# Graph passes: six of the 416 gathered tiles go through the SyncE queue, row by row

## The chip, the cores and the metric

One NeuronCore of a Trainium2 chip runs the whole program in one launch. The metric is the time of one execution on the device, in microseconds (us), as the median of several runs. PE is TensorE, DVE is VectorE, ACT is ScalarE, POOL is GpSimd, SP is SyncE. SP does no arithmetic here: it issues transfers and waits for semaphores.

## The reference

The model is a chain of four residual blocks over 3125 nodes of 256 features and 53,125 edges. The change is in the third block, a graph network of five layers:

```python
for l in range(L):                      # L = 5
    xl = h @ W[l] + b[l]
    ee = edge_attr @ We[l] + be[l]
    msg = norm * jax.nn.relu(xl[row] + ee)
    agg = jnp.zeros_like(xl).at[col].add(msg)
    conv = agg + jax.nn.relu(xl + root[l]) / deg[:, None]
    ...                                 # batch norm over the nodes, relu, residual
```

Each layer therefore gathers one row of `xl` for each edge (`xl[row]`), adds the edge's own product, and adds the result up by target node.

## The kernel before

The edges are sorted by target and padded to 416 tiles (`ET`) of 128 edges. A layer is one graph pass, `graph_layer_edges`. It has 26 iterations (`ITERS`) of 16 tiles (`BODY`), and the tiles are worked two at a time: pair `u` of an iteration is tiles `2u` and `2u+1`. The first pass ("opening") reads a table of 258 columns (`xl_table`, `XROW`), whose last two columns are weights of the node; the other four read `xl_rows` with 256 columns, and run inside a loop over the layers.

The engines work side by side in one block and are ordered by semaphores that count tiles or pairs:

- POOL, `gather(n)`: for each of the two tiles of pair `n` one indirect transfer fetches 128 rows into buffer `g.g[:, j]`, where `j` is the tile's place in its iteration. There are 16 buffers. From the ninth pair on it first waits until the pair that last used the buffers has been summed (`g.summed`). Its loop is written out in full (208 pairs).
- SP: `load_features` brings the edge features of half an iteration (8 tiles, 512 KB) into `g.ea[:, q]`. The load for half `q` of the next iteration waits until PE has made the products of half `q` of this one (`g.product`), so each load is asked for about half an iteration ahead of its use. The first two loads are made before the pass.
- PE: `products` multiplies the features of a pair with `We` into PSUM, two pairs ahead; `sums` multiplies messages with a one-hot matrix (the sum by target).
- DVE: `add_pair` (L2523) adds gathered rows and product; `add_sums` (L2544) adds the sums to `agg`; once an iteration it loads 16 register values with `lagging_bases` (L154).
- ACT: the relu of the messages and half of the one-hot matrices. In the first pass DVE also copies weights out of the gathered tiles for each half (`keep_half`, `g.kept`), and POOL waits for that copy before it reuses the buffers.

SP's part of the pass is these lines:

```python
with sp.Fori(0, ITERS - 1) as it:
    at = [places(q, it + 1) for q in range(2)]
    used = [sp.snap(it * (BODY // 2) + HALF // 2 * (q + 1)) for q in range(2)]
    for q in range(2):
        sp.wait_ge(g.product, used[q])
        load_features(q, at[q])
```

Of the kernel before, what the change touches and what calls it, by code (L numbers as in the profile page):

```python
# [42 lines left out]
SCORE_WINDOW = 2  # L43
LAYERS = 5
XROW = D + 2
PARTS = 3
EA = PARTS * PARTS * 4
ED = 128
# [1943 lines left out]
def graph_first_inputs(k):  # L1992
# [7 lines left out]
    with ExitStack() as c:  # L2000
# [11 lines left out]
        @block.sync  # L2012
        def _(sp):
            def load_x(i):
                sp.dma_start(k.x[:, i * STEP:(i + 1) * STEP, :], tile_rows(k.sum_d, i * STEP, STEP)).then_inc(x_in[i], 16)

            load_x(0)
            sp.dma_start(w[:], a["g1_w"][0:P, :].rearrange("p (b d) -> p b d", b=K)).then_inc(g.weights, 16)
            sp.dma_start(g.bias[:], a["g1_bias"][0:1, :].broadcast_to([P, 2 * D])).then_inc(g.weights, 16)
            sp.dma_start(g.cols[:], a["g1_cols"][0:P, :]).then_inc(g.weights, 16)  # L2020
            sp.dma_start(g.we[:], a["g1_we"][0:P, :]).then_inc(g.weights, 16)
            for i in range(1, NSTEP):
                load_x(i)
            sp.wait_ge(done, 1)
            sp.dma_start(k.deg_d, k.deg[:]).then_inc(stored, 16)
            load_first_half_tiles(k, sp)
            sp.wait_ge(stored, 16)
            sp.dma_start(k.dinv_row[:, 0:NP], k.deg_d.rearrange("t p -> (t p)").unsqueeze(0).broadcast_to([P, NP])
                         ).then_inc(stored, 16)
            sp.wait_ge(ready, 2)  # L2030
            with nc.allow_non_contiguous_dma(reason="two numbers for each row of the table"):
                sp.dma_start(k.xl_table[:, D:XROW].rearrange("(t p) c -> p t c", p=P), cols[:]
                             ).then_inc(stored, 16)
            for s in range(NSTEP):
                sp.wait_ge(g.biased, STEP * (s + 1))
                sp.dma_start(tile_rows(k.xl_table, s * STEP, STEP, 0, D), row[:, s % 2, :, :]).then_inc(g.stored[s % 2], 16)
            sp.wait_ge(stored, 48)
            for s in range(2):
                sp.wait_ge(g.stored[s], 16 * ((NSTEP + 1 - s) // 2))

# [317 lines left out]
def graph_layer_edges(k, l, nodes=None):  # L2358
# [13 lines left out]
    @block.sync  # L2372
    def _(sp):
        if nodes:
            nodes.sync(sp)

        def places(q, it):
            return a["ea128"][:, bass.ds(it * (BODY * P) + q * HALF * P, HALF * P)]

        def load_features(q, of_ea):  # L2380
            sp.dma_start(g.ea[:, q, :], of_ea).then_inc(g.ea_in[q], 16)

        with sp.Fori(0, ITERS - 1) as it:
            at = [places(q, it + 1) for q in range(2)]
            used = [sp.snap(it * (BODY // 2) + HALF // 2 * (q + 1)) for q in range(2)]
            for q in range(2):
                sp.wait_ge(g.product, used[q])
                load_features(q, at[q])

        for s in g.of_nodes:  # L2390
            sp.sem_clear(s)
        sp.wait_ge(g.added, ET + SB)

    @block.gpsimd
    def _(pool):
        if nodes:
            nodes.gpsimd(pool)

        def gather(n):

            for t in (2 * n, 2 * n + 1):
                j = t % BODY
                nc.gpsimd.indirect_dma_start(  # L2403
                    out=g.g[:, j, 0:width], out_offset=None, in_=table[:, :],
                    in_offset=bass.IndirectOffsetOnAxis(ap=k.src_all[:, t:t + 1], axis=0)
                ).then_inc(g.src_in[j], 16)

        for n in range(ET // 2):
            if n >= BODY // 2:
                pool.wait_ge(g.summed, 2 * (n - BODY // 2 + 1) + BODY)  # L2410
            if opening and n >= BODY // 2 and n % (HALF // 2) == 0:
                pool.wait_ge(g.kept, (n - BODY // 2) // (HALF // 2) + 1)
            pool.sem_inc(g.begun, 1)
            gather(n)
# [93 lines left out]
    def _(dve):  # L2508
# [5 lines left out]
        dve.sem_inc(g.added, SB)  # L2514
        dve.sem_inc(g.started, 2)

        def add_pair(it, u, seen):
            dve.wait_ge(g.product, it * (BODY // 2) + u + 1)
            dve.wait_ge(g.src_in[2 * u], seen)
            dve.wait_ge(g.src_in[2 * u + 1], seen)  # L2520

            dve.wait_ge(g.summed, it * BODY + 2 * u + 2)
            nc.vector.tensor_tensor(g.msg[:, 2 * u:2 * u + 2, :], g.g[:, 2 * u:2 * u + 2, 0:D],  # L2523
                                    ep[u % EB][:, 0:2 * D].rearrange("p (a d) -> p a d", a=2), ALU.add
                                    ).then_inc(g.raw, 1)
# [32 lines left out]
                                        ).then_inc(g.started, 1)  # L2558
                dve.wait_ge(g.started, it * 2 + 4)

        def body(it, first):
            seen = it * 16 + l * (16 * ITERS) + 16
            for u in range(BODY // 2):
                if not opening:
                    dve.wait_ge(g.summed, it * BODY + 2 * u + 2)
                    hot_tile(it, 2 * u)
                add_pair(it, u, seen)
                if opening and u % (HALF // 2) == HALF // 2 - 1:
                    keep_half(it, u // (HALF // 2))
                if u == 0:  # L2570
                    bases = lagging_bases(k, dve, base_regs, it * BODY)
                for i in range(2):
                    if 2 * u >= LAG or not first:
                        add_sums(it * BODY + 2 * u - LAG, u - LAG // 2, i, bases[2 * u + i])
                    if i == 0 and opening:

                        hot_tile(it, 2 * u)
                    if u == BODY // 2 - 2 + i and i == 0:
                        start_tile(it, 0)
                if u == BODY // 2 - 1:  # L2580
                    start_tile(it, 1)

        body(0, True)
        with dve.Fori(1, ITERS) as it:
            body(it, False)
        for i, base in enumerate(lagging_bases(k, dve, base_regs[0:LAG], ET)):
            add_sums(ET - LAG + i // 2 * 2, (BODY - LAG + i) // 2, i % 2, base)
        dve.wait_ge(g.added, ET + SB)
# [4 lines left out]
class GraphLayers:  # L2593
# [3 lines left out]
    def __init__(self, k, c):  # L2597
        self.nc = nc = k.nc
        sem, sb, bank = makers(k, c, "g1")
        self.w, self.we = sb("w", [P, K, D]), sb("we", [P, D])  # L2600
        self.bias, self.rowb = sb("bias", [P, 2 * D]), sb("rowb", [P, D])
        self.cols, self.rootb = sb("cols", [P, 4 * K]), sb("rootb", [P, K])
        self.cols_before = sb("cols_before", [P, 4 * K])
        self.rows = sb("rows", [P, 2, STEP, D])
        self.start = sb("start", [P, K, P])
        self.ea = sb("ea", [P, 2, HALF * P])
        self.g, self.msg = sb("g", [P, BODY, XROW]), sb("msg", [P, BODY, D])
        self.away = sb("away", [P, 2, P])
        self.onehot = sb("onehot", [P, BODY, P])
        self.sums, self.squares = sb("sums", [P, K, len(MOMENTS)]), sb("squares", [P, K, len(MOMENTS)])  # L2610
        self.whole, self.centre = sb("whole", [P, 2, K]), sb("centre", [P, K])
        self.mv, self.scale = sb("mv", [P, K, 2]), sb("scale", [P, 2, K])
        self.banks = [bank(f"b{i}") for i in range(8)]
        self.src_in = [k.pool_sem(f"g1_src_in{j}") for j in range(BODY)]
        self.stored = [sem(f"stored{i}") for i in range(2)]
        self.ea_in = [sem(f"ea_in{i}") for i in range(2)]
        (self.weights, self.xl_ready, self.biased, self.summed_bias, self.cleared_agg, self.conv, self.stat, self.root,
         self.step, self.scaled, self.updated, self.swept, self.multiplied, self.centred, self.squared, self.folded) = nodes = [sem(n) for n in (
             "weights", "xl_ready", "biased", "summed_bias", "cleared_agg", "conv", "stat", "root",
             "step", "scaled", "updated", "swept", "multiplied", "centred", "squared", "folded")]  # L2620
        (self.xlt_ready, self.rooted, self.started, self.begun, self.raw, self.product, self.hot, self.relu, self.summed,
         self.added, self.act_hot, self.distance, self.kept) = edges = [sem(n) for n in (
             "xlt_ready", "rooted", "started", "begun", "raw", "product", "hot", "relu", "summed",
             "added", "act_hot", "distance", "kept")]
        self.of_nodes, self.of_edges = nodes + self.stored, edges

    def open(self):
# [20 lines left out]
def host_arrays(inp):  # L2648
# [8 lines left out]
    def blocks(v, n):  # L2657
# [9 lines left out]
        "dst_first": dst[::P][None],  # L2667
        "src_cols": src.reshape(ET, P).T,
        "dst_row": dst[None],
        "dst_chunk": dst.reshape(P, ET),  # L2670
        "dst_chunk_first": dst[::ET][None],
        "dst_chunk_last": dst[ET - 1::ET][None],
# [68 lines left out]
```

## Time and profile before

| | |
|---|---|
| median of 3 runs | 4794.87 us (4794.35 to 4799.63) |
| the profiled execution, its own time | 4788.7 us |
| its span, first to last instruction | 4786.9 us |
| the five graph passes with the node work between them | from about 1609 to about 4420 us of the span |
| gathers of those passes | 2080 (5 times 416) |
| mean granted TensorE clock | 0.929 of full speed |

Times of rows are microseconds from the start of the span unless marked ns. "SPq" or "ACTq" is the queue of an engine: its transfers and register instructions, which the page does not count as busy. A time "to landing" runs from the issue of a transfer to its arrival. A group's idle time is that of its engine just before each of its instructions, with what ended it; "issue" means that nothing the profile shows was waited for.

### The profile page before, as it was taken

To read this page: it belongs to the slowest core of one execution; us is meant where nothing else is said; L and a number is where in the kernel's file an instruction comes from. 1 tells how busy PE (TensorE), PEld (TensorE's weight loads), DVE (VectorE), ACT (ScalarE), POOL (GpSimd) and SP (SyncE) were. 2 spreads that over 40 slices of the span, in tenths; PEclk is the share of its full clock that TensorE was granted. 3 is DMA by queue.
4 is the path that set the end of the run, shared out by engine and by line. 5 is a ranking of instruction groups with operands and counts; after the bars stand their busy time and mean duration, and the time that the engine had idled before them with its cause. 6 is when DMAs were issued, how large, how long until landed. Compare 5 with 4: busy or idle time off the path is not lost. (4 is left out here: it accounts for less than half of the span.)

```text
span 4786.9 us, 92098 instructions
## 1 busy us (share of the span) xinstructions
PE 3832.5 (80%) x21812; PEld 3231.2 (67%) x21813; DVE 3006.4 (63%) x7234; ACT 2211.6 (46%) x4854; POOL 2929.9 (61%) x3190
## 2 busy tenths in 40 slices
PE   6999808868999788878888788887888878887598
PEld 4666507757888677767777677776777767776465
DVE  5666676663222666676677666766776766767544
ACT  3222227632332455564555555554555555555221
POOL 3777709813333477766777577775777757776142
PEclk9999959969999899989999999998999989999599
DMA  6888828726664555544555455554555545554332
GB/s 216 256 252 256 250 68 233 208 86 196 201 194 134 167 158 158 157 136 144 157 157 157 130 155 156 157 157 126 157 157 157 157 125 158 157 157 132 134 119 70
DMA packets 390478, 778.47 MB, mean 163 GB/s; under 512 B 174940, under 2 KB 230864, under 8 KB 373095
## 3 DMA queue, kind: packets, MB, share of 16 engines
q1 hardware_dynamic: 244113, 401.10, 26.6%
q0 software_dynamic: 135168, 356.72, 26.1%
q10 hardware_dynamic: 11094, 19.50, 1.2%
q8 instruction: 37, 0.61, 0.1%
q14 instruction: 66, 0.54, 0.0%
HBM read 665.34 MB, written 113.43 MB: 163 GB/s over the span
## 5 line engine op out<-in xcount | busy, mean ns | idle before, releaser
L2403 POOL DMA_INDIRECT g_g<-xl_rows,src_all x1664 | 1579.2, 949 | 532.6 <-issue 440.5
L2428 PE MATMUL g_b<-g_we,g_ea 128*128 128x256 f32 x4160 | 1166.2, 404 | 448.2 <-DVE g_msg L2523 436.8
L2441 PEld LDWEIGHTS g_b<-g_onehot,g_msg 128*128 128x128 f32 x8320 | 1118.5, 198 | 124.3 <-DVE agg L2544 34.2
L2441 PE MATMUL g_b<-g_onehot,g_msg 128*128 128x128 f32 x8320 | 1143.4, 282 | 37.0 <-DVE agg L2544 19.3
L2428 PEld LDWEIGHTS g_b<-g_we,g_ea 128*128 128x128 f32 x4160 | 733.4, 196 | 605.4 <-DVE g_msg L2523 531.2
L2505 ACT ACTIVATE g_msg<-g_msg 128x512 f32<-128x512 f32 x1040 | 653.3, 628 | 826.6 <-DVE g_msg L2523 824.8
L2544 DVE TENSOR_TENSOR agg<-agg,g_b 128x256 f32 x2080 | 867.9, 417 | 261.5 <-issue 131.6
L2523 DVE TENSOR_TENSOR g_msg<-g_g,g_b 128x512 f32<-128x512 f32 x1040 | 711.5, 684 | 487.0 <-DMA g_g<-xl_rows,src_all 318.7
L2485 ACT ACTIVATE g_away<-iota_row,dst_rel 128x128 f32<-128x128 f32 x1040 | 405.9, 390 | 209.9 <-DMA g_g<-xl_table,src_all 132.8
L2403 POOL DMA_INDIRECT g_g<-xl_table,src_all x416 | 395.1, 950 | 168.1 <-issue 113.6
L513 POOL DMA_INDIRECT sc_g<-h_table,sc_idx x416 | 404.6, 973 | 132.9 <-issue 116.7
L2490 ACT ACTIVATE g_onehot<-g_away,pos_w,neg_w 128x128 f32<-128x128 f32 x832 | 410.5, 493 | 110.7
L545 PE MATMUL sc_pe_h<-ae_h_rows,sc_onehot 128*128 x1664 | 427.9, 401 | 40.5 <-DVE sc_prod L650 40.5
L545 PEld LDWEIGHTS sc_pe_h<-ae_h_rows,sc_onehot 128*128 128x128 f32 x1664 | 300.6, 190 | 127.9 <-issue 86.7
L2530 DVE TENSOR_SCALAR g_onehot<-iota_row,dst_rel,pos_w 128x128 f32<-128x128 f32 x832 | 296.7, 357 | 65.7 <-PE g_b L2441 45.4
L870 POOL TENSOR_TENSOR at_msg<-at_g,at_attn 128x256 f32<-128x256 f32 x416 | 242.4, 616 | 140.9 <-DMA at_g<-e_rows 110.4
L588 ACT ACTIVATE sc_enc<-sc_pe_e 128x512 f32<-128x512 f32 x208 | 118.8, 598 | 425.1 <-PE sc_pe_e L534 406.0
L951 PE MATMUL at_ps<-at_onehot,at_msg 128*128 128x128 f32 x1664 | 236.8, 292 | 84.7 <-POOL at_msg L870 41.9
L951 PEld LDWEIGHTS at_ps<-at_onehot,at_msg 128*128 128x128 f32 x1664 | 209.2, 200 | 112.2 <-POOL at_msg L870 86.4
L1950 POOL DMA_INDIRECT sum_d<-ex_y,ex_give x56 | 99.9, 1785 | 266.5 <-DVE ex_y L1907 161.9
L1861 ACT ACTIVATE ex_hid<-ex_hp,ex_b 128x256 f32<-128x256 f32 (+1 forms) x256 | 114.4, 447 | 301.7 <-PE ex_hp L1819 297.7
L967 DVE TENSOR_TENSOR agg<-agg,at_ps 128x256 f32 x416 | 175.5, 422 | 120.5 <-PE at_ps L951 80.2
(359 smaller groups left out, 4291.2 us busy)
## 6 DMA issues: line engine op xcount, KB each, us to landing
g_ea<-in_ea SPq DMA_DIRECT2D x260, 512.0 KB
ex_w<-in_f_w SPq DMA_DIRECT2D x80, 1024.0 KB, 6.6
e_rows<-sc_g SPq DMA_DIRECT2D x52, 1088.0 KB, 5.1
at_g<-e_rows SPq DMA_DIRECT2D x104, 544.0 KB, 4.5
g_g<-xl_rows,src_all POOLq DMA_INDIRECT x1664, 2.8
sc_rel<-rel_row ACTq DMA_DIRECT2D x52, 256.0 KB, 5.0
xl_rows<-g_rows SPq DMA_DIRECT2D x16, 640.0 KB, 3.3
sc_g<-h_table,sc_idx POOLq DMA_INDIRECT x416, 4.0
```

The source lines that it names most:

```text
L513: nc.gpsimd.indirect_dma_start(out=g[:, j, :], out_offset=None, in_=k.h_table[:, :], in_offset=bass.IndirectOffsetOnAxis(ap=idx[:, q, j % ...
L545: last = nc.tensor.matmul(pe_h[u % HB][:, i, 0:HROW], onehot[:, q, b, (at + i) * P:(at + i + 1) * P], k.h_rows[:, bass.ds(blocks[2 * u + i ...
L951: last = nc.tensor.matmul(ps[u][:, at:at + P], msg[:, j, b * P:(b + 1) * P], onehot[:, j, :], start=True, stop=True)
L2403: nc.gpsimd.indirect_dma_start(out=g.g[:, j, 0:width], out_offset=None, in_=table[:, :], in_offset=bass.IndirectOffsetOnAxis(ap=k.src_all[ ...
L2428: last = nc.tensor.matmul(ep[u % EB][:, i * D:(i + 1) * D], g.ea[:, q, (at + i) * P:(at + i + 1) * P], g.we[:], start=True, stop=True)
L2441: last = nc.tensor.matmul(ps[u % (SB // 2)][:, at:at + P], g.msg[:, j, b * P:(b + 1) * P], g.onehot[:, j, :], start=True, stop=True)
L2485: nc.scalar.activation(g.away[:, j // 2 % 2, :], k.iota_row[:], ACT.Abs, bias=k.dst_rel[:, bass.ds(it * BODY + j, 1)], scale=-1.0).then_in ...
L2490: nc.scalar.activation(g.onehot[:, j, :], g.away[:, j // 2 % 2, :], ACT.Relu, bias=bias, scale=scale).then_inc(g.act_hot, 1)
L2505: nc.scalar.activation(m, m, ACT.Relu).then_inc(g.relu, 1)
L2523: nc.vector.tensor_tensor(g.msg[:, 2 * u:2 * u + 2, :], g.g[:, 2 * u:2 * u + 2, 0:D], ep[u % EB][:, 0:2 * D].rearrange("p (a d) -> p a d", ...
L2530: nc.vector.tensor_scalar(g.onehot[:, j, :], k.iota_row[:], k.dst_rel[:, at], weight, ALU.is_equal, ALU.mult).then_inc(g.hot, 1)
L2544: nc.vector.tensor_tensor(window, window, ps[u % (SB // 2)][:, i * D:(i + 1) * D] .rearrange("p (b n) -> p b n", b=K), ALU.add).then_inc(g ...
```

## The change

SP takes over one tile in every fourth iteration: tiles 80, 144, 208, 272, 336 and 400 of each pass, each the first tile of its iteration (buffer 0 of `g.g`). A new tile `g.fetched` holds 128 rows; a new host array `src_sp` lists the 768 source indices. SP's loop becomes six turns (`SP_TURNS`) of four iterations. After each of the eight feature loads of a turn, `fetch_rows` loads 16 indices into registers and issues 16 transfers of one row each. At the end of the turn `hand_over` waits for all 128 rows, waits until buffer 0 is free (in the first pass also for `keep_half`), copies `g.fetched` to the buffer in one local transfer, and waits for that. POOL leaves the six tiles out, but keeps its waits. DVE's wait for buffer 0 counts POOL's gathers and the handed tiles separately, and its loop is cut differently: five iterations written out, a loop of five rounds of four iterations, and one more written out.

```diff
+SP_ROWS = 16
+SP_TURN = P // SP_ROWS // 2
+SP_TURNS = (ITERS - 2) // SP_TURN
+def sp_tile(turn):
+    return (SP_TURN * turn + SP_TURN + 1) * BODY
...
-            sp.wait_ge(stored, 48)
+            sp.dma_start(g.sp_src[:], a["src_sp"]).then_inc(stored, 16)
+            sp.wait_ge(stored, 64)
...
+        row_regs = [sp.alloc_register(f"g1_{tag}_row{i}") for i in range(SP_ROWS)]
+        def fetch_rows(turn, half):
+            sp.load(row_regs, g.sp_src[0:1, bass.ds(turn * P + half * SP_ROWS, SP_ROWS)])
+            rows = [sp.snap(r, min_val=0, max_val=NP - 1) for r in row_regs]
+            for i, n in enumerate(rows):
+                p = half * SP_ROWS + i
+                sp.dma_start(g.fetched[p:p + 1, 0:width], table[bass.ds(n, 1), 0:width]).then_inc(g.row_in, 16)
+        def features(it, q):
+            at = places(q, it + 1)
+            used = sp.snap(it * (BODY // 2) + HALF // 2 * (q + 1))
+            sp.wait_ge(g.product, used)
+            load_features(q, at)
+        def hand_over(turn):
+            it = turn * SP_TURN + SP_TURN
+            landed, copied = sp.snap(turn * (P * 16) + P * 16), sp.snap(turn * 16 + 16)
+            free, kept = sp.snap(it * BODY + (BODY + 2)), sp.snap(it * 2 + 1)
+            sp.wait_ge(g.row_in, landed)
+            sp.wait_ge(g.summed, free)
+            if opening:
+                sp.wait_ge(g.kept, kept)
+            sp.dma_start(g.g[:, 0, 0:width], g.fetched[:, 0:width]).then_inc(g.handed, 16)
+            sp.wait_ge(g.handed, copied)
+            sp.sem_inc(g.passed, 1)
-        with sp.Fori(0, ITERS - 1) as it:
+        with sp.Fori(0, SP_TURNS) as turn:
+            for i in range(SP_TURN):
+                it = turn * SP_TURN + i
+                for q in range(2):
+                    features(it, q)
+                    half = 2 * i + q
+                    fetch_rows(turn, half)
+            hand_over(turn)
+        for it in range(SP_TURNS * SP_TURN, ITERS - 1):
             for q in range(2):
-                sp.wait_ge(g.product, used[q])
-                load_features(q, at[q])
+                features(it, q)
...
+        by_sp = [sp_tile(turn) for turn in range(SP_TURNS)]
         def gather(n):
             for t in (2 * n, 2 * n + 1):
                 j = t % BODY
+                if t in by_sp:
+                    continue
...
-            dve.wait_ge(g.src_in[2 * u], seen)
+            if u:
+                dve.wait_ge(g.src_in[2 * u], seen)
+            else:
+                dve.wait_ge(g.src_in[0], by_pool * 16 + l * (16 * (ITERS - SP_TURNS)))
+                if by_sp is not None:
+                    dve.wait_ge(g.handed, by_sp * 16)
...
-        body(0, True)
-        with dve.Fori(1, ITERS) as it:
-            body(it, False)
+        START = SP_TURN + 1
+        for it in range(START):
+            body(it, it == 0, it + 1, None)
+        with dve.Fori(0, SP_TURNS - 1) as turn:
+            for i in range(SP_TURN):
+                body(turn * SP_TURN + (START + i), False, turn * (SP_TURN - 1) + (START + i), turn + 1)
+        for it in range((SP_TURNS - 1) * SP_TURN + START, ITERS):
+            body(it, False, it + 1 - SP_TURNS, SP_TURNS)
```

## Rows read from the trace of the kernel before

**Rows 1.** The page: busy time of each engine, and the DMA engines' busy tenths.

```profile
PE 3832.5 (80%) x21812; PEld 3231.2 (67%) x21813; DVE 3006.4 (63%) x7234; ACT 2211.6 (46%) x4854; POOL 2929.9 (61%) x3190
...
DMA  6888828726664555544555455554555545554332
```

**Rows 2.** The page, costliest groups: busy us, mean ns, idle us before and its releasers.

```profile
L2403 POOL DMA_INDIRECT g_g<-xl_rows,src_all x1664 | 1579.2, 949 | 532.6 <-issue 440.5
L2428 PE MATMUL g_b<-g_we,g_ea 128*128 128x256 f32 x4160 | 1166.2, 404 | 448.2 <-DVE g_msg L2523 436.8
...
L2523 DVE TENSOR_TENSOR g_msg<-g_g,g_b 128x512 f32<-128x512 f32 x1040 | 711.5, 684 | 487.0 <-DMA g_g<-xl_rows,src_all 318.7
```

**Rows 3.** Timeline of POOL, last gathers of pass five: start, us, idle before.

```profile
4410.06 0.95 POOL L2403 DMA_INDIRECT g_g<-xl_rows,src_all  x1 [0.30 <-issue]
4411.31 0.95 POOL L2403 DMA_INDIRECT g_g<-xl_rows,src_all  x1 [0.30 <-issue]
```

**Rows 4.** Gathers and feature loads of pass five: ns min/median/max, first and last start.

```profile
L2403 POOL DMA_INDIRECT g_g<-xl_rows,src_all x416: 942/946/1168, 3890.9 to 4411.3; - x139
...
L2381 SPq DMA_DIRECT2D g_ea<-in_ea x50: 332/333/360, 3901.3 to 4391.5; - x50
```

**Rows 5.** Waits of SP's queue: us in total, times, longest.

```profile
SPq L2381 <- PE g_b L2428: 2259.1, 243, 13.4
```

**Rows 6.** The last but one feature load of pass five, and DVE's last sum.

```profile
L2381 SPq DMA_DIRECT2D g_ea<-in_ea x1: 333/333/333, 4383.6 to 4383.6; - x1
...
4419.96 0.42 DVE L2544 TENSOR_TENSOR agg<-agg,g_b 128x256 f32 x1 [0.20 <-DVE agg L2544]
```

**Rows 7.** Timeline of DVE, late in pass five: two adds with no wait between.

```profile
4403.65 0.68 DVE L2523 TENSOR_TENSOR g_msg<-g_g,g_b 128x512 f32<-128x512 f32 x1
...
4405.38 0.68 DVE L2523 TENSOR_TENSOR g_msg<-g_g,g_b 128x512 f32<-128x512 f32 x1
```

**Rows 8.** SP's queue: transfers with an address from a register, timeline and instructions.

```profile
4571.77 0.33 SPq L1507 DMA_DIRECT2D ex_w<-in_f_w  x1
4572.28 0.33 SPq L1508 DMA_DIRECT2D ex_b<-in_f_b  x1
...
L1508 SPq FUSED_REGOPS  x8: 37/37/37, 4510.9 to 4715.9; - x8
L1508 SPq MOVE ex_b<-in_f_b x8: 29/29/29, 4511.0 to 4716.0; - x8
...
L2381 SPq FUSED_REGOPS  x250: 37/44/51, 1619.0 to 4391.3; - x125
```

**Rows 9.** Issues of one-partition loads by ACT's queue, and four-partition stores by SP's.

```profile
6.85 0.30 ACTq L380 DMA_DIRECT2D base_row<-in_dst_first  x1
7.18 0.27 ACTq L381 DMA_DIRECT2D base_lag<-in_dst_first  x1
...
L230 SPq DMA_DIRECT2D ew_parts<-tab_ew_part x9: 600/601/742, 26.7 to 49.9; - x9
```

**Rows 10.** Register loads: DVE's of 16 or 4 values, SP's of one, PE's of 16.

```profile
L154 DVEq TENSOR_LOAD <-base_lag x162: 349/1100/1352, 705.7 to 4417.4; - x162
...
L1502 SPq TENSOR_LOAD <-group_expert x8: 262/272/466, 4509.5 to 4661.2; - x8
...
L552 PEldq TENSOR_LOAD <-block_row x26: 1122/2282/2558, 67.0 to 573.8; - x26
```

**Rows 11.** DMA issues: times, KB each, median us from issue to landing.

```profile
at_g<-e_rows SPq DMA_DIRECT2D x104, 544.0 KB, 4.5
...
xl_rows<-g_rows SPq DMA_DIRECT2D x4, 128.0 KB, 2.4
...
g_cols_before<-in_g_cols SPq DMA_DIRECT2D x4, 4.0 KB, 1.7
```

**Rows 12.** DVE's first instruction after a pass: with the layer loop's jump, and without.

```profile
2711.25 0.69 DVE L2185 SCALAR_TENSOR_TENSOR agg<-agg,dinv_row 128x512 f32<-128x512 f32 x1 [1.02 <-PEq L2632]
...
4421.07 0.69 DVE L2185 SCALAR_TENSOR_TENSOR agg<-agg,dinv_row 128x512 f32<-128x512 f32 x1 [0.69 <-PEq L2632]
```

More of the change, by code:

```diff
@@ L2381, in load_features @@
             sp.dma_start(g.ea[:, q, :], of_ea).then_inc(g.ea_in[q], 16)
-        with sp.Fori(0, ITERS - 1) as it:
-            at = [places(q, it + 1) for q in range(2)]
-            used = [sp.snap(it * (BODY // 2) + HALF // 2 * (q + 1)) for q in range(2)]
+        row_regs = [sp.alloc_register(f"g1_{tag}_row{i}") for i in range(SP_ROWS)]
[30 more added lines that the diff above has]
+        for it in range(SP_TURNS * SP_TURN, ITERS - 1):
             for q in range(2):
-                sp.wait_ge(g.product, used[q])
-                load_features(q, at[q])
+                features(it, q)
         for s in g.of_nodes:
@@ L2515, in _, with add_pair @@
         dve.sem_inc(g.started, 2)
-        def add_pair(it, u, seen):
+        def add_pair(it, u, seen, by_pool, by_sp):
             dve.wait_ge(g.product, it * (BODY // 2) + u + 1)
-            dve.wait_ge(g.src_in[2 * u], seen)
+            if u:
[4 more added lines that the diff above has]
+                    dve.wait_ge(g.handed, by_sp * 16)
             dve.wait_ge(g.src_in[2 * u + 1], seen)
@@ L2559, in start_tile, with body @@
                 dve.wait_ge(g.started, it * 2 + 4)
-        def body(it, first):
+        def body(it, first, by_pool, by_sp):
             seen = it * 16 + l * (16 * ITERS) + 16
@@ L2566, in body @@
                     hot_tile(it, 2 * u)
-                add_pair(it, u, seen)
+                add_pair(it, u, seen, by_pool, by_sp)
                 if opening and u % (HALF // 2) == HALF // 2 - 1:
@@ L2606, in __init__ @@
         self.ea = sb("ea", [P, 2, HALF * P])
+        self.fetched, self.sp_src = sb("fetched", [P, XROW]), sb("sp_src", [1, SP_TURNS * P], I32)
         self.g, self.msg = sb("g", [P, BODY, XROW]), sb("msg", [P, BODY, D])
@@ L2621, in __init__ @@
         (self.xlt_ready, self.rooted, self.started, self.begun, self.raw, self.product, self.hot, self.relu, self.summed,
-         self.added, self.act_hot, self.distance, self.kept) = edges = [sem(n) for n in (
+         self.added, self.act_hot, self.distance, self.kept, self.row_in, self.handed, self.passed) = edges = [sem(n) for n in (
              "xlt_ready", "rooted", "started", "begun", "raw", "product", "hot", "relu", "summed",
-             "added", "act_hot", "distance", "kept")]
+             "added", "act_hot", "distance", "kept", "row_in", "handed", "passed")]
         self.of_nodes, self.of_edges = nodes + self.stored, edges
@@ L2669, in host_arrays @@
         "dst_row": dst[None],
+        "src_sp": np.concatenate([src[sp_tile(n) * P:sp_tile(n) * P + P] for n in range(SP_TURNS)])[None],
         "dst_chunk": dst.reshape(P, ET),
```

## The prediction

> **What bounds the kernel now.** I read the page's busy shares first. No engine stands out over the whole span: PE is busy 80%, POOL 61% [rows 1]. Shares over seven stages say little about one stage, so I went to the groups of the graph passes. There the picture is plain. DVE's add of gathered rows waits 318.7 us for the gathers of passes two to five, PE's products wait 436.8 us for that add, and POOL, which issues the gathers, waits almost only for its own issue: 440.5 of 532.6 us of idle time [rows 2]. The timeline shows its beat: one gather every 1.25 us, 0.95 of work and 0.30 of issue [rows 3]. Pass five has 416 gathers from 3890.9 to 4411.3, which is 520.4 us over 415 steps, or 1.254 us a gather [rows 4]. That is 20.06 us for the 16 tiles of an iteration. DVE alone would be faster: late in the pass two adds stand 1.73 us apart [rows 7], where POOL needs 2.51 us for the pair. With the register load and the start tile at an iteration's edge I put DVE's own iteration near 17 us, so about 3 us of each iteration are spare on it.
>
> SP is nearly idle. It waits 2259.1 us for PE's products in the five passes [rows 5] and has one feature load to issue every 10 us.
>
> **What the change can win.** Six gathers a pass fewer on the engine that sets the pace: 6 × 1.254 = 7.5 us a pass, 37.6 us over five passes. Nothing else is removed, so this is also the ceiling. POOL keeps the wait in front of the shortened pairs, which costs nothing as long as its buffers come free early. They do, since few of its waits are for PE.
>
> **What SP has to do for it.** A turn is four iterations. POOL will take 63 × 1.254 = 79.0 us for it. In that time SP must issue eight feature loads, eight register loads, 128 row transfers and one hand-over. Each is priced from rows:
>
> - A transfer with a register address is three instructions on SP: one to compute the offset (37 to 51 ns), a move (29 ns) and the issue. Two such transfers of 128 partitions start 0.51 us apart, 0.333 + 0.037 + 0.029 plus 0.11 for three gaps between instructions, 0.037 each [rows 8].
> - A row transfer writes one partition. The trace has two issues of that shape, on ACT's queue with fixed addresses: 0.30 and 0.27 us [rows 9]. I take 0.275, since the first came out of a crowded burst. With 0.11 of gaps, 0.049 for the offset instruction near its upper end and 0.029 for the move, a row costs r = 0.464 us. The bounds: 0.45 with the 37 ns offset instruction, and 0.524 if the issue costs the 0.333 of 128 partitions with the 51 ns one. Further out lies 0.60 for a transfer of four partitions [rows 9], which would make r = 0.79. I take the near row because it has the same shape, one partition from one contiguous row.
> - The register load of 16 values: DVE's takes 1.10 at the median, and 0.35 for four values, which is 0.0625 a value; SP's own load of one value takes 0.27 [rows 10]. Together 0.27 + 15 × 0.0625 = 1.21. The upper bound is PE's 2.28 for 16 values [rows 10].
> - Feature load 0.52, two register instructions for index and count 0.15, address of the register load 0.08, gap 0.04. With the register load this makes 2.0 us in each half.
>
> So a half costs c = 2.0 + 16 × 0.464 = 9.42 us, beside the 10.0 us that POOL gives it. The hand-over comes on top: the last row lands 1.4 us after its issue ends (a small load takes 1.7 from its start), the copy of 128 KB lands 2.4 after its issue [rows 11], and semaphores, counts and the jump back make 0.6, of which the jump is 0.33: the layer loop's jump lengthens DVE's gap from 0.69 to 1.02 us [rows 12]. Hand-over: 4.4 us. A turn of SP is T = 8 × 9.42 + 4.4 = 79.8 us, against POOL's 79.0. SP runs practically at POOL's pace.
>
> The Trainium skill (Runtime: NRT & Kernel Launch, Instruction fetch mechanics) says that a taken branch to code outside the small window that the engine holds stalls for a fetch. SP's turn is some 450 instructions long and DVE's loop body becomes four times as long, so by that rule both pay at each jump. The jump over a whole pass in this trace costs the 0.33 us above, and I go by that.
>
> **Where SP's lag would be felt.** What waits behind these 128 issues is the next feature load, and behind that PE's products. The load is asked for when PE has finished the products of the half, and first needed five pairs later, 5 × 2.51 = 12.5 us; a 544 KB load of the earlier stage lands in 4.5 us [rows 11], so I take 4 for this one, and 8.5 us are spare. The hand-over's 4.4 us fit into that, and 0.6 us a half come back. Over the pass: the first feature load goes out 10.4 us after the first gather [rows 4]. After six turns SP is free at X = 10.4 + 6 × 79.8 = 489 us for the last but one. Before, that one went out at 492.7 [rows 6], and it will be wanted at 486 if POOL is five gathers ahead by then. It is 3 us late with 8.5 to spare. From a late load to the end of the pass DVE needs about 24 us: 4 to land, 0.9 for product and start, seven pairs of 1.74, 1.6 for the edge and 5.4 from the last add to the last sum. The pass now ends at 4420.4 − 3890.9 = 529.5 us [rows 6] and should end at 522. So the full gain holds while X stays below 498, T below 81.3 and r below 0.476; the change breaks even at X = 505.5, T = 82.5, r = 0.485; beyond, each 0.01 us on a row costs 7.7 us a pass (6 × 128 × 0.01).
>
> In the first pass the hand-over also waits for DVE's copy of the weights of the first half of the iteration, some 6 us later than the buffer's first pair is summed. SP then stands about 7 us late with its next feature load, still under 8.5, and makes it up over the eight halves.
>
> **The other parts.** DVE gets one more wait and a few register instructions of 0.04 us in an iteration; its 3 spare us cover them, and without that cover they would cost under 0.2 us an iteration, 26 us in all. The 3 KB index load stands behind the last table store, whose landing is waited for anyway. The row transfers move 128 KB in 80 us, small beside DMA engines that are about half busy in these stages [rows 1], and they are waited for by SP alone. The copy reaches buffer 0 about ten us before DVE reads it. All three are costed at nothing.
>
> **Sum.** 4788.7 us (the profiled execution's own time) − 5 × 7.5 = 4751.1. The median of the runs is 6.2 above that execution, so 4757.3 us against 4794.9.
>
> **Rivals.**
> *SP becomes the bound.* The place is the 16 row issues of a half, the point r = 0.485. For it: the margin is 0.02 us on a price taken from two issues on another queue. At r = 0.524, T = 87.5, X = 535, the pass ends at 559, 29.7 us later than now: +148, so 4943 us. The register load at PE's price instead gives c = 10.5, T = 88.4 and +35 a pass: 4970 us. Against it: the one-partition rows, and that SP's load of a single value is cheap. 0.29.
> *Rows are dear outright*, as the four-partition stores: c = 14.6, T = 121.5, X = 739, the pass ends at 763: +1168, so about 5960 us. 0.05.
> *Only the first pass suffers.* Its rows have 258 elements, not 256, and might be split otherwise than the 416 of the near row. At r = 0.79 in this pass alone: +234 − 30, 4999 us; at 0.52, near 4795. 0.07. The Trainium skill (DMA: Bandwidth & Descriptors, Why a DMA increments its semaphore by 16 and not by 1) has a transfer run on the largest number of engines up to 16 that divides its slowest dimension, 16 for 256 and 6 for 258, and the issuing queue write the missing increments itself; no row here shows what that costs.
> *The gain goes elsewhere.* T lies between 81.3 and 82.5, or late feature loads after each hand-over eat what POOL saves: within 0.2% of now, 4795 us. 0.11.
> The forecast has 0.48.
>
> **How the numbers follow.** A change under 0.2% (9.6 us) can't be told from none in this kernel. Faster: the forecast, and 0.03 of the cases that lose part of the gain: 0.51. Same: what is left of the in-between cases and the mild end of the first-pass case, 0.10. Slower: 0.39. The range goes from 4750 (the full gain, and the spread of the runs) to 4975 (SP bound by either price); outside lie the dear rows and the worst of the first pass and of SP's case, 0.15 to 0.2. The forecast's own range is 4750 to 4775.
>
> **What would show it.** Row transfers on SP that start 0.46 us apart; register loads near 1.2 us; 2050 gathers at a 1.25 us beat; SP still waiting for PE's products before most feature loads; PE's products not waiting for a feature load; passes of about 522 us from the first gather to the last sum. The prediction is wrong if rows start over 0.48 us apart: then SP no longer waits for products, PE waits for feature loads, POOL waits for PE's sums, and the pass stretches by 6 turns of whatever SP needs.

## The result and the profile after

The change made the kernel faster: 4766.7 us (median of 4, 4764.63 to 4768.19) against 4794.95 us, ratio 0.9942, 95% interval 0.993 to 0.9954. The gain is 28.2 us; 37.6 were forecast. The profiled execution took 4765.28 us, its span is 4763.5.

The page of the changed kernel, its costliest groups and two of its queues of packets (queue: packets, MB, share of 16 engines):

```profile
PE 3822.2 (80%) x21812; PEld 3231.1 (68%) x21813; DVE 3018.3 (63%) x7234; ACT 2211.9 (46%) x4854; POOL 2904.6 (61%) x3160
...
q14 instruction: 378, 3.10, 0.2%
...
L2450 POOL DMA_INDIRECT g_g<-xl_rows,src_all x1640 | 1557.7, 950 | 525.9 <-issue 427.5
L2475 PE MATMUL g_b<-g_we,g_ea 128*128 128x256 f32 x4160 | 1163.5, 404 | 427.9 <-DVE g_msg L2575 372.7
...
L2575 DVE TENSOR_TENSOR g_msg<-g_g,g_b 128x512 f32<-128x512 f32 x1040 | 712.2, 685 | 402.9 <-DMA g_g<-xl_rows,src_all 239.2
```

These answer [rows 2]. POOL's group of the later passes has 24 gathers fewer at 950 ns each (949 before), and POOL still waits almost only for its own issue. DVE's add of gathered rows waits 239.2 us for gathers where it waited 318.7. Pass five, gathers and last sum (ns min/median/max, first and last start):

```profile
L2450 POOL DMA_INDIRECT g_g<-xl_rows,src_all x410: 942/946/1176, 3873.6 to 4387.0; - x137
```
```profile
L2596 DVE TENSOR_TENSOR agg<-agg,g_b x3: 421/423/424, 4394.8 to 4396.0; 128x256 f32 x3
```

The gathers take 513.4 us where they took 520.4 [rows 4], and from the first gather to the end of the last sum it is 522.8 us against 529.5 [rows 6].

SP's new work: row transfers of later passes and of the first, the register load, the two instructions behind it that check the indices, the feature load, and the copy of the hand-over:

```profile
L2400 SPq MOVE g_fetched<-xl_rows x3072: 29/29/42, 2187.0 to 4360.2; - x192
L2400 SPq DMA_DIRECT2D g_fetched<-xl_rows x3072: 224/228/319, 2187.1 to 4360.2; - x192
...
L2400 SPq DMA_DIRECT2D g_fetched<-xl_table x768: 224/228/294, 1621.6 to 2097.0; - x192
```
```profile
L2396 SPq TENSOR_LOAD <-g_sp_src x240: 1131/1143/1181, 1619.8 to 4352.3; - x120
```
```profile
L2397 SPq FUSED_REGOPS  x480: 161/175/198, 1621.1 to 4353.7; - x160
```
```profile
L2390 SPq DMA_DIRECT2D g_ea<-in_ea x250: 357/364/380, 1619.3 to 4368.1; - x125
```
```profile
L2417 SPq DMA_DIRECT2D g_g<-g_fetched x30: 497/508/561, 1702.9 to 4361.6; - x30
```

SP's timeline over one half in which it waits for nothing, and over a hand-over; then the loop's branch in that hand-over and the instruction after it:

```profile
3317.38 0.37 SPq L2390 DMA_DIRECT2D g_ea<-in_ea  x1
3319.56 6.49 SPq L2400 DMA_DIRECT2D g_fetched<-xl_rows  x16
3326.31 0.36 SPq L2390 DMA_DIRECT2D g_ea<-in_ea  x1
```
```profile
3393.79 1.87 SPq L2400 DMA_DIRECT2D g_fetched<-xl_rows  x5
3396.99 0.51 SPq L2417 DMA_DIRECT2D g_g<-g_fetched  x1
3402.93 0.37 SPq L2390 DMA_DIRECT2D g_ea<-in_ea  x1
```
```profile
L2421 SPq COMPARE_BRANCH  x1: 45/45/45, 3399.8 to 3399.8; - x1
L2421 SPq FUSED_REGOPS  x1: 59/59/59, 3402.7 to 3402.7; - x1
```

This half takes 8.93 us, start to start of the feature loads. The sixteen rows start (6.49 − 0.23)/15 = 0.417 us apart. From the last row's issue to the next feature load it is 3402.93 − 3395.66 = 7.3 us, of which 2.9 lie between the branch and the next instruction. So T = 8 × 8.93 + 7.3 = 78.7 us from these rows. The whole trace puts it a little higher: halves in which SP waits for nothing last 8.9 to 9.3 us, and the second to fifth turns of the five passes last 78.8 to 81.8, 79.5 at the median, counted between feature loads. SP runs at POOL's pace of 79.0, not inside it. The jump back occurs only five times in a pass: there the branch is followed by 2.4 to 3.2 us without an instruction, 2.8 at the median of 25; behind the sixth turn, where the loop ends, it is 0.05. What is left of SP's and PE's waits (us in total, times, longest; these answer [rows 5]):

```profile
SPq L2390 <- PE g_b L2475: 117.8, 39, 13.4
```
```profile
PE g_b L2475 <- DMA g_ea<-in_ea: 43.4, 19, 4.2
```

SP waited for products 243 times, now 39 times. PE waits for a feature load 19 times in five passes; before, its list of waits has none of these.

DVE around the end of pass three, the last sum and the first instruction of the node work, which answers the first row of [rows 12]:

```profile
3262.54 0.42 DVE L2596 TENSOR_TENSOR agg<-agg,g_b 128x256 f32 x1 [0.20 <-DVE agg L2596]
3266.73 0.69 DVE L2194 SCALAR_TENSOR_TENSOR agg<-agg,dinv_row 128x512 f32<-128x512 f32 x1 [3.77 <-issue]
```

Here a new stall shows, waiting for nothing the profile knows. DVE's own loop over the iterations has it too: in passes two to five four stalls each of 3.2 to 5.1 us, as many as that loop has jumps back. Its waits in pass four (us in total, times, longest):

```profile
DVE g_onehot L2582 <- issue: 16.8, 6, 5.1
```

The table below sets both profiled executions side by side, worked out from the starts of gathers and sums; a pass runs from the first gather to the start of the last sum, "between" from there to the next pass's first gather:

| us | pass 1 | 2 | 3 | 4 | 5 | sum | between | sum |
|---|---|---|---|---|---|---|---|---|
| before | 529.6 | 529.3 | 528.9 | 528.9 | 529.1 | 2645.8 | 41.6, 41.1, 41.1, 41.1 | 164.9 |
| after | 523.2 | 521.3 | 522.2 | 522.3 | 522.4 | 2611.4 | 41.8, 44.5, 44.5, 44.3 | 175.1 |

The passes give 34.4 us, and 10.2 are given back between them, all at the three places where the layer loop jumps back. That leaves 24.2 us, and the two executions differ by 23.4.

### The profile page after: what moved, and what is told of

Read it like the earlier page. It is cut to its first block and busy times, and to the rows that moved or that the text cites. A ratio compares the mean times of both kernels' runs of the same rounds, so it can differ in the third digit from the quotient of the medians.

```text
span 4763.5 us, 103541 instructions
## 1 busy us (share of the span) xinstructions
PE 3822.2 (80%) x21812; PEld 3231.1 (68%) x21813; DVE 3018.3 (63%) x7234; ACT 2211.9 (46%) x4854; POOL 2904.6 (61%) x3160
## 5 line engine op out<-in xcount | busy, mean ns | idle before, releaser
L2450 POOL DMA_INDIRECT g_g<-xl_rows,src_all x1640 | 1557.7, 950 | 525.9 <-issue 427.5
L2575 DVE TENSOR_TENSOR g_msg<-g_g,g_b 128x512 f32<-128x512 f32 x1040 | 712.2, 685 | 402.9 <-DMA g_g<-xl_rows,src_all 239.2
L975 DVE TENSOR_TENSOR agg<-agg,at_ps 128x256 f32 x416 | 175.6, 422 | 120.2 <-PE at_ps L959 79.5
```

Source lines behind the costliest of these rows:

```text
L2450: nc.gpsimd.indirect_dma_start(out=g.g[:, j, 0:width], out_offset=None, in_=table[:, :], in_offset=bass.IndirectOffsetOnAxis(ap=k.src_all[ ...
```

## The experiments

The theory after the result: SP keeps up with POOL as forecast, and what is missing is the price of longer code in the layer loop, on DVE above all. The rival: the fill itself, its transfers and SP's queue, costs the difference. All diffs are against the changed kernel unless said otherwise. Each time stands against runs of the kernel before on the same chip, taken together with it: 4796.51 us for the first four kernels (the first set), 4793.48 for the others (the second set). A kernel's gap is DVE's idle time from the last sum of a pass to the node work.

**SP's work alone.** POOL gathers all 416 tiles, DVE has its old loop, SP fetches all rows and copies the tile to a spare one.

```diff
-                if t in by_sp:
-                    continue
...
-            sp.dma_start(g.g[:, 0, 0:width], g.fetched[:, 0:width]).then_inc(g.handed, 16)
+            sp.dma_start(g.spare[:, 0:width], g.fetched[:, 0:width]).then_inc(g.handed, 16)
```

> POOL gathers all 416 tiles and DVE's loop is the old one; SP does all its new work, but copies the fetched tile into a spare one that nobody reads. Nothing is taken from POOL, so each pass should last 529 to 530 us from the first gather to the last sum, as before. Theory (code of DVE): the 3.3 us that the changed kernel loses at each of the three jumps back of the layer loop come from DVE's longer code; here DVE's gap at the jump is 1.0 us as before and the time is that of before, 4795 us, within 3. Rival 1 (code of SP): SP's turn of some 450 instructions is what is fetched anew; the gap is near 3.8 us and the time 10 us over before, 4805. Rival 2 (the row transfers disturb the gathers or the feature loads): the passes themselves get longer, by 1 us each or more.

Measured: 4801.51 us, ratio 1.001 (1.0 to 1.0019), +5.0 us. Its passes sum to 2652.4 us, 1.3 more each than before, and DVE's gap after a pass stays at 1.0. So the theory's 4795 within 3 was missed, rival 1's gap did not come, and rival 2's sign is there: the passes are longer. The size is uncertain. The two profiled executions differ by 9.8 us, of which 6.6 lie in the passes and 2.2 between them; the medians differ by only 5.0. SP's own first loads after pass three, though, come late and far apart:

```profile
3287.61 0.34 SPq L2283 DMA_DIRECT2D g_cols_before<-in_g_cols  x1
3289.51 0.34 SPq L2284 DMA_DIRECT2D g_w<-in_g_w  x1
```

The last sum ended at 3284.3, so the first load goes out 3.3 us later and the second 1.9 after that. In the kernel before, these were 0.9 and 0.54 us: the same stall at the same jump, now on SP. Most of it is hidden, since the time between passes grew by only 2.2 us in all.

**DVE's new loop alone.** POOL gathers all tiles and SP has its old loop; DVE runs the long cut with the old waits.

```diff
-            if u:
-                dve.wait_ge(g.src_in[2 * u], seen)
-            else:
-                dve.wait_ge(g.src_in[0], by_pool * 16 + l * (16 * (ITERS - SP_TURNS)))
-                if by_sp is not None:
-                    dve.wait_ge(g.handed, by_sp * 16)
+            dve.wait_ge(g.src_in[2 * u], seen)
```

> POOL gathers all tiles, SP is the old one; only DVE's loop is cut as in the changed kernel (five iterations written out, a loop of four, one written out). Passes last 529 to 530 us. Theory (code of DVE): the gap at the three jumps is 3.8 us instead of 1.0 and the time is 8 to 10 us over before, 4803 to 4805; stalls of DVE at the jumps inside a pass show as idle time ended by issue, up to 4 us each, and are covered by the gathers. Rival 1 (code of SP): the gap stays 1.0 and the time is 4795.

Measured: 4805.48 us, 1.0017 (1.0008 to 1.0026), +9.0 us. The passes are as before (2644.5 in all), and the loss stands between them:

```profile
3285.35 0.42 DVE L2584 TENSOR_TENSOR agg<-agg,g_b 128x256 f32 x1 [0.20 <-DVE agg L2584]
3289.27 0.69 DVE L2194 SCALAR_TENSOR_TENSOR agg<-agg,dinv_row 128x512 f32<-128x512 f32 x1 [3.50 <-issue]
```

This is the theory's forecast, gap and time. The passes do not pay although DVE stalls in them four times each, for 3.2 to 4.1 us. The instruction packets rise with it, from 66 in the kernel before:

```profile
q14 instruction: 228, 1.87, 0.1%
```

**Six tiles left out, nobody fills them.** SP has its old loop, DVE does not wait for handed tiles: it adds whatever stands in buffer 0 for these six tiles. The rest is the changed kernel.

```diff
-                if by_sp is not None:
-                    dve.wait_ge(g.handed, by_sp * 16)
```

> POOL leaves the six tiles of a pass out and nobody fetches them: their messages are computed from the rows that buffer 0 still holds. SP is the old one, DVE's loop is that of the changed kernel. This is the ceiling of what leaving the gathers out can give: 30 x 1.254 = 37.6 us less in the passes. Theory (code of DVE): with three jumps at 3.3 us more, 28 us under before, 4767, the same as the changed kernel within 2 us, so that SP's filling is free. Rival 1 (code of SP): no loss at the jumps, 4757. Rival 2 (the filling disturbs): 4760 to 4764.

Measured: 4764.82 us, 0.9933 (0.9919 to 0.9946), −31.7 us. DVE's gaps are 3.66, 3.45 and 3.49 us, as after. The gain is 3.7 us more than the theory's 28 and lies at the near edge of rival 2's range (31 to 35 under 4795), so this run speaks against a filling that is free.

**A shorter cut of DVE's loop.** Two nested loops and the first and last iteration written out: three copies of the body in place of ten.

```diff
+        body(0, True, 1, 0)
+        with dve.Fori(0, SP_TURNS) as turn:
+            with dve.Fori(0, SP_TURN) as i:
+                it = turn * SP_TURN + i + 1
+                body(it, False, turn * (SP_TURN - 1) + i + 2, turn)
+        body(ITERS - 1, False, ITERS - SP_TURNS, SP_TURNS)
```

> The changed kernel with the same work, but DVE's loop is two nested loops around one iteration, with one iteration written out on either side (the count of handed tiles starts at 16, so that every iteration can wait for it). SP is that of the changed kernel. Theory (code of DVE): the gap at the three jumps falls back to 1.0 us and the time is 10 us under the changed kernel, 4757. Rival 1 (code of SP): the gap stays 3.8 us and the time 4767. Rival 2: as rival 1, since neither the transfers nor the hand-over change.

Measured: 4772.34 us, 0.9944 (0.993 to 0.9958). The theory in this form fell: DVE's gaps are 3.68, 3.64 and 3.71 us, as long as with ten copies, and each pass is about 1.3 us longer than the changed kernel's (2618.1 in all). What did go away are the stalls inside the passes: none of the 3 us kind is left. Less code of this amount buys nothing at the layer loop's jump. Either length was not the cause, or three copies are already too long.

**DVE's loop as short as before.** One written-out iteration and one loop over 25, as in the kernel before. The turn and the place in it are computed from the count, and the handed tiles are counted from one on, so that every iteration can have the same wait.

```diff
+        body(0, True, 1, 0)
+        with dve.Fori(1, ITERS) as it:
+            turn = dve.snap((it - 1) // SP_TURN)
+            left = dve.snap((it - 1) % SP_TURN)
+            body(it, False, turn * (SP_TURN - 1) + left + 2, turn)
...
-                if by_sp is not None:
-                    dve.wait_ge(g.handed, by_sp * 16)
+                dve.wait_ge(g.handed, by_sp * 16 + 16)
```

> The changed kernel with DVE's loop in the shape that it had before the change: one iteration written out, then one loop over the other 25. The number of handed tiles is worked out from the iteration by a division in registers. DVE's code for a layer is then 4 entries longer than before the change, in the program listing, where the kernel with nested loops has some 60 more and the changed kernel over 560. The nested form kept the long gap, so the theory is now: the length of DVE's code within the layer loop decides, and one more iteration written out is already too much. By it the gap at the three jumps is 1.0 us again, each start of a pass comes 3.3 us earlier, and the time is 8 to 10 us under the changed kernel, near 4758. Rival (SP's long turn makes the gap together with something in DVE that any new count brings): the gap stays at 3.7 us and the time at 4767.

Measured: 4760.81 us (4758.68 to 4762.35), 0.9932 (0.9918 to 0.9945), −32.7 us. It is faster than both kernels. The gap is back at its old size:

```profile
3263.34 0.42 DVE L2596 TENSOR_TENSOR agg<-agg,g_b 128x256 f32 x1 [0.20 <-DVE agg L2596]
3264.77 0.69 DVE L2194 SCALAR_TENSOR_TENSOR agg<-agg,dinv_row 128x512 f32<-128x512 f32 x1 [1.00 <-PEq L2687]
```

**The changed kernel again**, in the second set, so that the two stand side by side.

> The changed kernel once more, on the same chip as the others of this call, so that they can be set against it. Both theories: 0.994 of before, 4767 us; gaps of 3.7 us at the three jumps.

Measured: 4767.51 us (4766.03 to 4769.67), 0.9946 (0.9932 to 0.9959), gaps 3.57, 3.54 and 3.65. The short loop wins 6.7 us, and no run of the one overlaps a run of the other.

**Four more rows in each half**, into a spare tile: SP's work made longer, nothing else.

```diff
+            for i in range(MORE):
+                sp.dma_start(g.spare[half * MORE + i:half * MORE + i + 1, 0:width],
+                             table[bass.ds(rows[i], 1), 0:width]).then_inc(g.row_in, 16)
```

> The changed kernel with four more row transfers in each half iteration, into a spare tile that nobody reads; the hand-over waits for them too. It asks how near SP is to being the bound. In the changed kernel a row costs 0.415 us, a half without waits 8.93 us and the hand-over with its jump 7.3 us, so a turn needs 78.7 us beside POOL's 79.0. Theory (SP has no room left): four rows more make a half 10.6 us, a turn 92.0, SP is free 10.4 + 6 x 92.0 = 562 us into the pass and the pass ends at about 586 instead of 522: 64 us more in each of five passes, 320 in all, 5085 us. Rival (the lag of SP is hidden by the buffers ahead of it, and what it costs is only the transfers' own interference): under 20 us more in all, 4785.

Measured: 5019.24 us, 1.0467 (1.0451 to 1.0483). SP's timeline, feature loads a half apart:

```profile
3483.24 0.36 SPq L2392 DMA_DIRECT2D g_ea<-in_ea  x1
3485.41 6.46 SPq L2402 DMA_DIRECT2D g_fetched<-xl_rows  x16
3491.96 1.19 SPq L2404 DMA_DIRECT2D g_spare<-xl_rows  x4
3493.45 0.36 SPq L2392 DMA_DIRECT2D g_ea<-in_ea  x1
```

And who waits now, PE and POOL:

```profile
PE g_b L2480 <- DMA g_ea<-in_ea: 562.0, 179, 11.7
```
```profile
POOL g_g L2455 <- PE g_b L2493: 285.5, 269, 9.7
```

It is the picture that the prediction drew for SP as the bound: PE waits for feature loads, POOL for PE's sums. Over the four halves to 3524.75 a half takes 10.38 us, so T = 8 × 10.38 + 7.3 = 90.3; the turns of the trace, from copy to copy, last 89.3 to 90.9. From the forecast's edge of 81.3 that makes 6 × 9.0 = 54 us a pass; measured were (5019.24 − 4767.51)/5 = 50.3. The rival, under 20 us in all, fell. The theory's 5085 us was 66 too high, mainly because it gave the half 10.6 us: the four added rows reuse indices at hand, have no offset instruction, and start only 0.32 us apart.

**Nobody fills, and the short loop.** The six tiles left out as above, SP's old loop, DVE's loop of the fifth experiment: the whole gain with neither price. Its edit is those two together.

> POOL leaves the six tiles out and nobody fetches them; SP is the old one and DVE has the single loop with the division. It leaves out the messages' own rows of those tiles (buffer 0's old rows are used). This is the gain with neither the fill nor the longer code. Theory (length of DVE's code): 37.6 us under before, 4757 to 4759, and 10 us under the same kernel with the cut loop. If the run with the single loop and SP's fill comes to the same time, the fill is free; the run with SP alone suggests that the fill costs 1 us a pass, so 5 us. Rival (SP's code): the same, since SP is the old one here.

Measured: 4754.24 us, 0.9919 (0.9906 to 0.9933), −39.2 us, gaps 1.02, 1.00 and 1.00. Instruction packets are back at the old count:

```profile
q14 instruction: 66, 0.54, 0.0%
```

**What arrives in the stall.** The traces also record the 8 KB packets of the instruction queue (q14) with their times. In the first 3.3 us after the last sum of passes two, three and four, the kernel before and the last kernel have one such packet. The three kernels with only DVE's or only SP's code long enough to stall (DVE's new loop alone, nobody fills with the long loop, SP's work alone) have two, and so has the one with SP's fill and DVE's short loop. The changed kernel and the one with nested loops, where both stall, have three. It is the same at each of the three jumps. Behind each of SP's 25 jumps back inside the passes one starts within 0.9 to 1.7 us of the branch. So code is being brought in during these stalls. Which engine a packet is for, the trace does not say; that follows from the counts.

**Put together.** Each price has three measurements, from kernels that differ in it alone. DVE's longer loop: +9.0 (alone), 7.5 (nobody fills: −31.7 against −39.2, across the two sets), 6.7 (the changed kernel against its short loop). The fill with SP's code: +5.0 (alone), 6.6 (short loop: −32.7 against −39.2), 5.7 (long loop: −26.0 against −31.7, across the two sets). Four of the six are differences around one square of kernels, so their sums are bound to agree; the two measured alone are the test. The ceiling of 39.2 less 9.0 and 5.0 leaves 25.2, and the changed kernel gained 26.0 and 28.2. Single differences here are as large as their intervals (0.13% is 6 us), but all six have the same sign and lie near each other. The trace shows where DVE's part lies. Of the fill's part it shows less: with the fill, where POOL leaves the tiles out, the passes are 0.6 us longer each with the long loop and 0.4 with the short one, and between passes it is 0.3 and 2.9 us more in all.

The granted clock is no rival for the cause. It is 0.931 to 0.936 in the runs with SP's work alone, which are slower than before (0.925 to 0.931), and 0.929 to 0.933 with nested loops, which have the full gap.

## Why the prediction was right

**What bounds the passes.** Right. Six gathers fewer were worth 39.2 us where nothing else was charged, forecast 37.6.

**SP's turn.** T was put at 79.8 us and is 78.7 by the rows shown, 79.5 at the median. That it came so close is luck in part, for three terms were off and cancel. A row costs 0.417, not 0.464: the issue of one partition takes 228 ns against the 275 taken from [rows 9]. The register load is 1.14 (1.21 forecast), but two instructions of 175 ns behind it, for the index check, were overlooked. A half is 8.93 instead of 9.42. The hand-over is 7.3 instead of 4.4, since the jump inside it costs 2.9 where 0.33 was taken. Had the row come at the forecast price with this hand-over, T would have been 82.7, past the break-even point.

**The margin.** Right in the length of the passes, which are 522 us as forecast; the last feature load but one goes out 490 to 493 us into a pass, where the forecast had SP free at 489. Two of the forecast's signs did not come: SP was to wait for products before most feature loads and waited before 39 of 250, and PE was not to wait for a feature load and waited 43.4 us in all. A turn as long as POOL's leaves SP nothing to wait for, so the first of these signs did not fit the forecast's own T. The run with four more rows shows that the margin was real and thin, and confirms the slope behind it within a tenth.

**The first pass.** That rival fell: its rows of 258 elements are issued in 228 ns like the later passes' rows, and its pass is 523.2 us. It is about 1 us longer than the others, in a kernel in which nobody fills too (522.7 against 520.9 to 522.0), so the fill is not the reason.

**The step that was mis-sized.** The total fell 9.4 us short of the forecast's gain, at a place where the forecast had put almost nothing: "The jump over a whole pass in this trace costs the 0.33 us above, and I go by that", and DVE's longer loop costed at nothing behind its 3 spare us. Inside a pass the cover held: DVE stalls up to 5.1 us at a time, 16.8 us in pass four, and the gathers hide it, for the passes lost nothing when DVE's new loop ran alone. Between passes there is no cover. There the gap went from 1.0 to 3.6 us on average, three times, plus what follows from it: 7 to 9 us. The 0.33 us was the price of a jump in a program of the old length, and the change altered that length. The other part of the shortfall is the fill, 5 to 7 us by the medians: longer passes, by 1.3 us when done alone and by about 0.5 where POOL leaves the tiles out, and SP's own late start at the three jumps. Which part of the pass time is contention and which is queueing was not separated. The two parts together are 12 to 16 us, and the ceiling was 1.6 above its forecast, which leaves 10 to 14 us missing; measured were 9.4 and, in the second set, 11.6.

The Trainium skill (Runtime: NRT & Kernel Launch, Instruction fetch mechanics) says that a taken branch to code outside the held window has to fetch it. The runs agree: packets of instructions went from 66 to 378, and 66 again with short code on both engines, and they arrive in the stalls. Following the rule would have helped the forecast only in part. Three DVE gaps longer by 2.6 us bring the forecast to 4765 us, close to what was measured. But SP's jump at 2.9 us in place of 0.33, in the forecast's sum as it stood, makes T = 82.4, at the break-even point, and a time near 4790 even before DVE's part. What kept the gain are the cheaper rows, which the forecast had not foreseen.

**Left open.** How long the code may be before the gap appears. DVE's part of the layer loop, counted in the built programs with its waits and branches, has 289 entries before, 295 with the short loop, 387 with three copies and 1083 after; the gap is there at 387. (The 4, some 60 and over 560 entries more that an expectation above names are counted without the waits.) In the nested kernel the inner jumps, over 119 entries, cost nothing visible. Whether the length alone decides, or also where the code lies, was not tried, nor why the nested loops cost 1.3 us a pass. Nor do the rows say what fills the stall behind the packet's arrival.

## What to carry over

An idle queue can take work off the engine that sets the pace, but price it over a whole turn, hand-over and jump included, for a margin of 1% is decided by the issue cost of the cheapest repeated step. Written-out iterations were not free in this kernel: keep a loop's body single by computing counts from its index and by starting a semaphore at a value that makes every wait the same. A jump's price read from a trace holds for code of that length only.

## What was not expected of the hardware

- A transfer of one row with a register address is issued in 228 ns, against 333 ns for the feature load's 128 partitions before the change and 364 after it, and such rows follow each other every 0.417 us.
- A jump back over SP's turn, 448 executed instructions, costs 2.4 to 3.2 us in which SP does nothing. On DVE the gap at the layer loop's jump is 3.4 to 3.8 us with the longer code and 1.0 with the short one.
- An 8 KB instruction packet starts 0.9 to 1.7 us after each such branch of SP, inside the stall.
- A register load of 16 values takes SP 1.14 us, half of PE's 2.28 [rows 10].
